# Order of VectorE's statistics, box sums and output additions at the end of layer 3, in a four-layer convolution kernel

## The reference, cut to what matters

```python
x = x + L0(gn(x))   # offsets by a 3x3 convolution, bilinear sampling, depthwise 3x3, pointwise
x = x + L1(gn(x))   # avg_pool3, 27 offset/mask channels by a 3x3 convolution, deformable 3x3 convolution
x = x + L2(gn(x))   # 3x3 convolution with prepared weights
x = x + L3(gn(x))   # two dynamic 1-D filters, a spatial and a channel gate (sigmoids), a 1x1 output product
```

## Time and profile before

| | before |
|---|---|
| median of 3 runs (range) | 1944.85 us (1942.91 to 1944.91) |
| profiled execution: its own time | 1943.77 us |
| profiled execution: span, first to last instruction | 1941.9 us |
| busy share of PE, DVE, ACT, POOL | 88%, 61%, 31%, 4% |
| mean granted TensorE clock | 0.949 |
| HBM traffic | 12.19 MB read, 8.39 MB written |

### The profile page before, as it was taken

One profiled execution on the slowest core, in us unless ns is written; L12 is line 12 of the kernel. 1 busy time (PEld: TensorE's weight loads), 2 busy tenths in 40 slices (PEclk: granted clock), 3 DMA queues, 4 the chain that ended last, 5 costly groups with the idle time before them and its releaser, 6 DMA issues.

```text
span 1941.9 us, 23888 instructions
## 1 busy us (share of the span) xinstructions
PE 1709.3 (88%) x7908; PEld 876.7 (45%) x7908; DVE 1186.2 (61%) x2227; ACT 602.5 (31%) x986; POOL 76.7 (4%) x92
## 2 busy tenths in 40 slices
PE   4968998889988899889997899978999789988976
PEld 2544543445435453355533545345543445435422
DVE  5275459654686347773487634985359654687356
ACT  2134132341324313243242422324123341324222
POOL 1010000000000000000000000010000000000000
PEclk8989999899999999899998999989999899999988
DMA  2000000000010000100001000010000100000000
GB/s 101 11 12 2 1 1 12 35 1 1 1 44 2 1 1 1 45 1 1 1 1 45 2 1 1 1 46 2 1 0 7 40 2 1 1 22 1 1 0 22
DMA packets 7120, 22.97 MB, mean 12 GB/s; under 512 B 1232, under 2 KB 1936, under 8 KB 6928
## 3 DMA queue, kind: packets, MB, share of 16 engines
q1 hardware_dynamic: 6928, 20.58, 2.9%
HBM read 12.19 MB, written 8.39 MB: 11 GB/s over the span
## 4 chain that ended last, share of the span: by engine, by line
issue 75%; PE 14%; DVE 5%; POOL 3%; ACT 2%; POOLq 0%; DVEq 0%; ACTq 0%
PE psN L462 3%; POOL gst L420 2%; PE psO L488 2%; PE psN L563 1%; PE psN L488 1%; PE psN L684 1%; PE psO L684 1%; POOL strip L428 1%; ACT xq L889 1%; PE ps L571 1%; PE psN L592 1%; PE psO L462 1%; DVE pool_v L1261 1%; DVE samp L1512 1%; PE psN L806 1%
## 5 line engine op out<-in xcount | busy, mean ns | idle before, releaser
L488 PE MATMUL psO<-samp,w 128*128 128x512 f32 x576 | 289.8, 635 | 20.8 <-ACT samp L889 20.8
L488 PE MATMUL psN<-xn,w 128*128 128x512 f32 x576 | 277.4, 605 | 5.9 <-issue 4.5
L592 PE MATMUL psN<-GQt,xq 64*128 64x144 f32 x2048 | 165.3, 300 | 25.9 <-ACT samp L889 25.5
L889 ACT ACTIVATE samp<-psN 128x576 f32<-128x576 f32 x256 | 152.7, 648 | 71.8 <-PE psN L592 71.8
L592 PEld LDWEIGHTS psN<-GQt,xq 64*128 64x128 f32 x2048 | 138.2, 186 | 55.9 <-ACT samp L889 42.1
L488 PEld LDWEIGHTS psO<-samp,w 128*128 128x128 f32 x576 | 106.0, 200 | 122.3 <-issue 110.5
L1052 ACT ACTIVATE samp<-psN,vec 128x512 f32<-128x512 f32 x160 | 110.0, 687 | 129.2 <-PE psN L806 129.2
L1209 DVE COPY xblk<-psN 120x256 f32<-120x256 f32 x128 | 54.3, 424 | 148.7 <-PE psN L528 148.5
L488 PEld LDWEIGHTS psN<-xn,w 128*128 128x128 f32 x576 | 98.8, 189 | 87.4 <-issue 85.1
L684 PE MATMUL psN<-img,w 128*128 128x512 f32 x288 | 134.1, 611 | 4.5 <-PE psO L546 4.5
L911 ACT ACTIVATE xn<-x,gst 128x1024 f32<-128x1024 f32 x32 | 40.3, 1259 | 308.8 <-DVE gst L1158 308.8
(11 more groups left out here) (142 smaller groups left out, 2304.8 us busy)
## 6 DMA issues: line engine op xcount, KB each, us to landing
xin<-in_x SPq DMA_DIRECT2D x16, 512.0 KB, 3.6
out<-yout SPq DMA_DIRECT2D x16, 512.0 KB, 2.8
w<-in_w SPq DMA_DIRECT2D x2, 576.0 KB, 5.5
samp<-in_r SPq DMA_DIRECT2D x1, 576.0 KB, 6.8
tab<-in_tab SPq DMA_DIRECT2D x1, 494.0 KB, 5.2
kh_w<-in_kh SPq DMA_DIRECT2D x1, 320.0 KB, 5.8
kv_w<-in_kv SPq DMA_DIRECT2D x1, 320.0 KB, 6.0
woT<-in_woT SPq DMA_DIRECT2D x1, 256.0 KB, 6.3
```

Of the source, the lines that this page charges most:

```text
L488: last = mm(dst[:, h, :], wgt[:, k, :], rhs(h, k), start=(k == 0), stop=(k == K9 - 1))
L592: last = mm(pair(u)[:, g, :].rearrange("p (k r c) -> p k r c", k=K9, c=SW)[:, :, :, cols], xQ[rows, t, a, e, :], w[rows, e, :, :, cols], s ...
L889: return nc.scalar.activation(out, in_, ACT.Copy)
```

## The change

1. VectorE takes the statistics of image 0 (`stats L1A`) before it waits for the spatial gate (ahead of `sm`), and no longer behind `wo2`.
2. `affine` is split into `affine_var` (to the request to GpSimd) and `affine_scale` (from GpSimd's answer on), and other work is put between the halves.
3. The four parts of image 0's box sum come before both output additions; after `store_ready(0)` come the four parts of image 1's, and `store_ready(1)` is last. `pool3` of image 1 waits for `pooled_ready` of image 0, since both use `pool_v`.
4. TensorE: `group_mean L1A` stands between the last-but-one and the last matmul of `fill`, and `group_mean L1B` before the last half of the output product (so far L1A stood before the first image's second half, and L1B behind everything).
5. TensorE at the head of a pass: `offset_parts(3)` waits for the first `y_ready` of the pass before, and only `blocks(0)` for both. For this `y_ready` starts at 2.

```diff
@@ signal @@
-        def signal(name, per_pass):
-            signals.append(Signal(sem(name), per_pass))
+        def signal(name, per_pass, start=1):
+            signals.append(Signal(sem(name), per_pass, start))
-        y_ready = signal("y_ready", 2)
+        y_ready = signal("y_ready", 2, 2)
@@ TensorE, head of a pass @@
-                pe.wait_ge(y_ready.sem, y_ready.at(i, 0))
+                pe.wait_ge(y_ready.sem, y_ready.at(i, -1))
                 pe.wait_ge(pooled_ready.sem, pooled_ready.at(i, 2))
                 offset_parts(3, img[1], w1off)
+
+                pe.wait_ge(y_ready.sem, y_ready.at(i, 0))
                 blocks(i, 0, range(TILES))
@@ TensorE, end of layer 3 @@
-                fill(33, 36)
+                fill(33, 35)
+                if more:
+                    group_mean(i, "L1A", order)
+                fill(35, 36)
...
-                        if h and more and s == 0:
-                            group_mean(i, "L1A", order)
+                        if h and more and s:
+                            group_mean(i, "L1B", order)
...
-                if more:
-                    group_mean(i, "L1B", order)
@@ VectorE: affine becomes affine_var and affine_scale, cut ahead of this wait @@
+            def affine_scale(own, name, order):
+                g = norm(name)
+                dve.wait_ge(rstd_ready.sem, rstd_ready.at(own.i, nth(name, order)))
...
+            def affine(own, name, order):
+                affine_var(own, name, order)
+                affine_scale(own, name, order)
@@ VectorE: pool3 @@
+                if part == 0 and s:
+
+                    dve.wait_ge(pooled_ready.sem, pooled_ready.at(i if order is FIRST else i + 1, 1))
@@ VectorE, end of layer 3 @@
+                if more:
+                    stats(own, "L1A", order)
+
                 dve.wait_ge(l3_act.sem, l3_act.at(i, P_GATE + 1))
                 v_.tensor_tensor(sm, sg, xc[:], ALU.mult).then_inc(l3_maps.sem, 1)
...
                 if more:
-                    stats(own, "L1A", order)
+                    affine_var(own, "L1A", order)
                     residual0(i + 1, 1)
-                    affine(own, "L1A", order)
+                    affine_scale(own, "L1A", order)
                     stats(own, "L1B", order)
+                    pool3(own, 0, 0, i, order)
+                    pool3(own, 0, 1, i, order)
+                    affine_var(own, "L1B", order)
+                    pool3(own, 0, 2, i, order)
+                    affine_scale(own, "L1B", order)
+                    pool3(own, 0, 3, i, order)
                 store_ready(0)
                 if more:
                     for part in range(4):
-                        pool3(own, 0, part, i, order)
+                        pool3(own, 1, part, i, order)
                 store_ready(1)
                 if more:
-                    affine(own, "L1B", order)
-                    for part in range(4):
-                        pool3(own, 1, part, i, order)
                     assert own.n == DVE_STEPS, own.n
```

More of the change, by code:

```diff
@@ L1138, in stats, with affine_var @@
                     .then_inc(stats_ready.sem, 1)
-            def affine(own, name, order):
+            def affine_var(own, name, order):
                 g = norm(name)
-                n = nth(name, order)
-                dve.wait_ge(group_ready.sem, group_ready.at(own.i, n))
+                dve.wait_ge(group_ready.sem, group_ready.at(own.i, nth(name, order)))
                 own.step(v_.tensor_copy(g[:, 14:16], ps[SAMPLE[name]][:, 0:2]))
@@ L1152, in affine @@
                     .then_inc(var_ready.sem, 1)
-                dve.wait_ge(rstd_ready.sem, rstd_ready.at(own.i, n))
+            def affine_scale(own, name, order):
+                g = norm(name)
+                dve.wait_ge(rstd_ready.sem, rstd_ready.at(own.i, nth(name, order)))
                 own.step(v_.tensor_scalar(g[:, 19:20], g[:, 18:19], 1.0 / 9 if name in ("L1A", "L1B") else 1.0, None,
```

## The result

The changed kernel takes 1909.36 us (median of 4 runs, 1908.28 to 1909.85), the kernel before, run beside it, 1943.88 us (4 runs): a ratio of 0.9824, 95% interval 0.9807 to 0.9841, or 34.5 us. Beside the three groups of experiments the kernel before came to 1940.2, 1941.4 and 1941.5 us; against these the gain would be 31 to 32 us. The forecast was 1921, range 1912 to 1935: right in direction, too small, and the time lies 2.6 us under the range.

A forecast was written before the change was run, and what follows sets the result against it. TensorE, 88% busy, bounds on the mean; its idle time at pass boundaries can be won. Six boundaries of 3.3 us (20) and 2.1 at the seventh make 22, with 2 for the clock 24: median 1921, range 1912 to 1935.

The forecast's parts named there:

- Statistics in the gate wait: VectorE ahead of the gate product: 1.80 us of statistics fill a 2.07 us wait, 0.27 us left, gate product not delayed.
- End of image 0's box sum: VectorE at the first boundary: box sum ends at 337.9 instead of 339.97, 2.1 us earlier; bounds 337.4 and 338.5.
- the signs of being wrong: GpSimd's answers hold VectorE, VectorE's branch comes behind the last output addition, or offset matmuls take 7.5 us each time.
- Strip copy: GpSimd's copy of 2.11 us beside part 0 of image 1's box sum: 0.9 us lost, bounds 0 and 2.1.
- Branch over the last output addition: VectorE's branch runs while the last output addition does; bias addition 3.1 to 3.2 us after part 3's start, at 347.1.
- Two level chains: VectorE ready at 347.1, TensorE at 347.05 to 348.6; the later decides, about 347.85 on the mean, against 351.17.
- The sum at the boundaries: Six boundaries of 3.3 us are 20, the seventh gains 2.1; together 22 us.
- 2 of 5 more for the clock: Offset matmuls at full clock would gain 5 us more in all; 2 were counted, making 24 us.
- Rival E: Slower by TensorE's clock at 0.5 from the first offset matmul on, matmuls 7.8 us; 1952, chance 0.05.
- The rest of the pass: Behind the bias addition: no gain in the forecast's sum; a rival had the gain given back there, 1944, chance 0.05.
- Rival C: Everything but the branch clears: no conflict, clock 1.0, strip copy without cost; 5.4 us a boundary, 1908, chance 0.06.

The follow-up runs named there:

- late strip copy: Changed kernel with GpSimd's strip copy of image 0 waiting for image 1's box sum as well; 1908.5 us.
- first output first: Changed kernel with the first output addition back ahead of image 0's box sum; 1914.5 us.
- The repeated matmuls: One matmul of layer 1's second convolution given out twice: changed kernel 1923.0 us, kernel before 1937.5 us; two given out twice in the changed kernel: 1919.6 us.
- either edit beyond the change alone: Changed kernel with three extra matmuls in TensorE's idle time (1911.5 us), or with GpSimd's strip copy behind image 1's box sum (1908.5 us); both, 1904.4 us.

## Why the prediction was wrong

Its mechanism at the boundary held; what failed is the part of the sum that stands for TensorE's clock in the rest of the kernel.

- *Statistics in the gate wait*: right, 0.27 us left over.
- *End of image 0's box sum*: forecast 2.1 us earlier with a conflict for GpSimd's power; measured 2.35 (11.97 against 14.32 us after the gate product). The conflict is real (1.46 us) and costs 0.44 us of waiting, which the prediction had both in its sum (0.5 us) and among the signs of being wrong. The step was 0.25 us too dear, about 1.5 us at six boundaries.
- *Strip copy*: forecast 0.9 us on one part, measured 1.1. The output addition is untouched: 1.28 us beside the copy, and 1.28 us without it in the kernel with the late strip copy. So is the residual, with 1.22 us beside image 0's power and 1.22 us in the kernel before.
- *Branch over the last output addition*: right; forecast 3.1 to 3.2 us after part 3's start, measured 3.26.
- *Two level chains*: right. The first boundary was forecast to give its bias addition at 347.1, 21.4 us after the gate product if VectorE decides; it was 21.3. TensorE's wait of 2.48 us for the bias addition shrank to under 0.5, as forecast, where TensorE decides; at the first boundary it is still 2.01.
- *The sum at the boundaries*: 22 us, and 2 of 5 more for the clock, 24; measured 26.5. The offset matmuls were put at their old times, 6.60 us on the mean; they took 4.61 once and 6.25 to 6.29 six times, so that this term of a boundary was 0.35 us too long at six of them. That full clock leaves them at least half of the 7.50 us was an estimate; at a granted clock of 1.00 they took 4.60 to 4.65 us. Rival E's 7.8 us for them at the low clock throughout was too short: the 4.61 us at a granted clock of 1.00 make 9.2 at 0.50, by my estimate; no group ran at 0.50 throughout, and the longest, 7.51 us with the first output first, had a mean of 0.60.
- *The rest of the pass*: this is the step that failed. "I count 2 of them: 24 us" priced the clock at the one group of matmuls next to the change, and left bodies, start and end at nothing, without a reason. They gave 7.8 us in the two profiled executions, where the boundaries alone, at 26.5 us, would have left about 1917 us, inside the range. The prediction had evidence against it in hand, matmuls that took 5.9 to 7.5 us in the same code from pass to pass, and read it as a spread of one term.

The repeated matmuls show that gains of this size need no better order: with the boundaries as they were (within 0.4 us), bodies and rest together moved from 1757.7 to 1771.7 us in the changed kernel for 6.8 us of work (7.2 beyond it), and in the kernel before from 1765.5 to 1760.1 (12.2 less than the work added). A neutral edit of this kind could have taken them away. What stays open: part of the rest is different from one execution to the next, since the start, up to the first bias addition of pass 0, took from 114.8 to 117.8 us over all fourteen profiles with no changed code in it; of the 3.2 us of the rest 1.9 lie there and 1.7 in the end (the stretches between took 0.4 more), and how much of this is chance can't be told from one profile of each. Rival C, nearly the measured time at 1908, had its number right for a wrong reason: both conflicts that it did without are there.

## What to carry to other kernels

When two engines take turns, follow both chains through the stretch and take the later at each end: here either edit beyond the change alone bought 2.1 or 2.5 us at the boundaries, and both together 8.6. An instruction that waits for nothing is worth trying last in a loop's body: here the last output addition ran beneath the 2.95 us of the branch, and ahead of the box sum it cost 1.2 us at the first boundary. A GpSimd operation is worth trying beside a VectorE instruction with one input in PSUM: beside the strip copy the output addition kept its 1.28 us, where an addition of two SBUF tiles took 2.39 instead of 1.28. And where TensorE's clock changes in every pass, here between 1.00 and 0.50, the error bar of a forecast is at least what a neutral change moves: here 6.8 us of repeated matmuls gave 4 us less in one kernel and 13.6 more in another, 7 to 11 us off their work, so a gain under that size should be read from the stretch that was edited, not from the total.

## What the runs showed of the hardware that was not expected

- A power of 128 x 1 elements on GpSimd takes 0.55 us alone and 1.46 us beside an addition of two SBUF tiles that had begun 0.16 us before it; it ends 0.40 us after the addition.
- A loop's branch on VectorE costs 2.8 to 3.1 us until the next instruction in the changed kernel, while the last output addition still runs beneath. In the kernel before with five extra matmuls it is 3.8 to 4.6 us at five of six boundaries, where loads of 1 MB were issued 1.2 to 2.1 us before the branch, and 2.8 us where they were issued 3.0 us before it.
- Adding 6.8 us of matmuls made the kernel before 4 us faster (0.9975, 0.9960 to 0.9989), and made the changed kernel 13.6 us slower.
